# Keys and values of two attentions projected inside an earlier feed-forward and passed through DRAM

## The chip, the cores and the metric

The kernel runs on one NeuronCore of a Trainium2 chip. The metric is the time of one execution in microseconds (us) on the device, lower is better. The engines are PE (TensorE, matrix products into PSUM), ACT (ScalarE), DVE (VectorE), POOL (GpSimd) and SP (SyncE, which only issues transfers); each runs its own instructions in order and waits for others by semaphores.

## The reference, cut to what matters

Eight layers in a row change `x` (16 sequences, 128 tokens, 256 features); four of them are attentions over the same `ctx_1024` (16, 128, 256):

```python
x = x + _L0_xattn_ref(_layernorm(x), ctx_1024, ctx_1024, ...)   # autocorrelation
x = x + _L0_ffn_ref(_layernorm(x), ...)                         # quantised feed-forward
x = x + _L1_xattn_ref(_layernorm(x), ctx_1024, ctx_1024, ...)   # attention one, |i - j| <= 64
x = x + _L1_ffn_ref(_layernorm(x), ...)                         # slots
x = x + _L2_xattn_ref(_layernorm(x), ctx_1024, ctx_1024, ...)   # attention two
x = x + _L2_ffn_ref(_layernorm(x), ...)                         # receptance
x = x + _L3_xattn_ref(_layernorm(x), ctx_1024, ctx_1024, ...)   # attention three, rotary
x = x + _L3_ffn_ref(_layernorm(x), ...)                         # routed experts
# in attentions one to three, 16 heads of 16 features:
Q = query @ Wq.T + bq;  K = key @ Wk.T + bk;  V = value @ Wv.T + bv
out = softmax(Q K^T / 4) V @ Wo.T + bo     # three: Q and K turned by the rotary tables first
```

The keys and values depend on `ctx_1024` and the weights alone, not on `x`. The quantised feed-forward rounds `x`, gate, up, silu(gate) and their product each to a grid whose step needs the largest magnitude of the whole tensor.

## The kernel before, in words

Each layer is one function with one block, and a barrier of all engines stands between blocks. Inside a block every engine's instructions are written out by hand in the order in which they run; each waits on named semaphores (`enough(engine, semaphore, count)`).

`attention(layer)` serves attentions one to three. Its **preamble** computes the layer norm (a chain of small DVE instructions over all 16 sequences), and then in four groups of four sequences: keys (`project_keys`, PE; `keys_out`, ACT, or for the rotary attention `plain_out` on ACT, `swap_halves` on PE and `rope` on DVE), values (`project_values`, PE; `values_out`, DVE), and the normalised `x` turned by PE (`turn_x`) and split in two float16 parts (`x_out` on ACT, `x_low` on DVE). Then come the queries, eight jobs of 128x512 (`project_queries`, `queries_out`; rotary: the same three steps as for keys). Its **loop** takes the 16 sequences, about one per pass, in a software pipeline: PE makes approximate float16 scores for the row maxima (`maxima`), DVE reduces them, PE turns the maxima (`turn_maxima`), makes the exact float32 scores (`scores`), subtracts the maxima (`shift`), ACT takes the exponentials (`exponentials`), PE weighs the values (`weigh_values`), turns the sums, and after DVE's division turns and projects the result (`turn_sums`, `turn_attended`, `output`). Attention one adds its window to both kinds of scores with eight small matmuls each (`add_window`). DVE also adds the output bias to X (`add_bias`).

`quantised_ffn` first makes gate and up (`hidden` on PE, `evict` on ACT), then quantises. That part is a chain of three maxima over everything: up (scale US), silu (SS), product (PS). Every scale ends on DVE (`finish_scale`); ACT rounds (`round_up`, `round_silu`), DVE multiplies (`product`) and takes maxima (`max_product`), and after scale PS ACT writes `product_parts` for PE's `output`. For US, PE turns DVE's partial maxima (`combine_up_maxima`).

`slot_ffn` is the longest stage; POOL has three memsets there and nothing else.

## Time and profile before

| | us |
|---|---|
| median of 3 runs (2041.72 to 2044.39) | 2043.6 |
| the profiled execution | 2044.04 |
| its span, first to last instruction | 2042.1 |
| quantised feed-forward, 124.5 to 320.3 | 195.8 |
| attention one, 320.3 to 470.4: preamble, loop | 44.7, 104.6 |
| slots, 470.4 to 1360.9 | 890.5 |
| attention two, 1360.9 to 1494.0: preamble, loop | 42.7, 90.4 |
| attention three, 1555.8 to 1724.7: preamble, loop | 76.2, 92.7 |
| routed experts, from 1724.7 | 317.4 |

Stages follow each other without overlap, so a stage's change is the kernel's change; the median stands 0.4 us below the profiled execution, and 1.9 us of that execution lie outside its span. Times in rows are from the start of the span. "Keys" and "L851" are names and lines of the kernel before.

### The profile page before, as it was taken

What the parts mean: (1) busy time and instruction counts of PE and PEld (TensorE: products, weight loads), DVE (VectorE), ACT (ScalarE), POOL (GpSimd) and SP (SyncE); (2) the same over time, 40 slices, a digit from 0 to 9 for tenths busy, and PEclk for the clock granted to TensorE, in tenths of its full rate; (3) what the DMA queues carried; (4) which work ended last, traced back from release to release, by engine and by line L of the source; (5) the groups of instructions that cost most, each with busy time, mean ns of one, the idle gap of its engine ahead of it and who ended that gap; (6) DMA issues with size and microseconds to landing.
All of it is one profiled execution on the core that took longest, in us unless ns stands there. A gap on an engine that the chain in (4) does not pass through costs nothing. (4 is left out here: it accounts for less than half of the span.)

```text
span 2042.1 us, 40835 instructions
## 1 busy us (share of the span) xinstructions
PE 1818.8 (89%) x16076; PEld 1319.7 (65%) x16076; DVE 1502.2 (74%) x3131; ACT 1148.0 (56%) x1942; POOL 207.6 (10%) x175
## 2 busy tenths in 40 slices
PE   7959358996799999999999999988988798699997
PEld 6844145665377777766767777755665466588886
DVE  6987887667777777777777777687766777688885
ACT  3535753556366666666666665535552555377774
POOL 0001400000000000000000000000000100156664
PEclk9979779998999999999999999999998999799999
DMA  6120001002100000000000000010001001778885
GB/s 223 47 79 1 0 0 53 2 3 94 42 22 22 22 22 22 22 22 22 22 22 22 22 1 1 1 52 2 3 21 56 1 3 49 211 235 240 249 254 117
DMA packets 85037, 117.54 MB, mean 58 GB/s; under 512 B 11760, under 2 KB 70576, under 8 KB 84720
## 3 DMA queue, kind: packets, MB, share of 16 engines
q1 hardware_dynamic: 76016, 102.82, 15.6%
q0 software_dynamic: 8832, 12.11, 2.9%
q8 instruction: 130, 2.13, 0.4%
q14 instruction: 59, 0.48, 0.1%
HBM read 99.95 MB, written 14.96 MB: 56 GB/s over the span
## 5 line engine op out<-in xcount | busy, mean ns | idle before, releaser
L2637 PE MATMUL sl_ps_eo<-sl_w,sl_hT 128*128 128x256 f16 x3072 | 353.1, 273 | 0.8 <-DVE sl_hT L2880 0.7
L2614 PE MATMUL sl_ps_h<-sl_slot_inT,sl_w 128*128 128x512 f16 x1536 | 338.1, 379 | 0.5 <-ACT sl_h L2757 0.5
L2637 PEld LDWEIGHTS sl_ps_eo<-sl_w,sl_hT 128*128 128x128 f16 x3072 | 298.2, 98 | 36.1 <-DVE sl_hT L2880 1.3
L2757 ACT ACTIVATE sl_h<-sl_ps_h,sl_b1T 128x512 f32<-128x512 f32 x256 | 175.7, 687 | 170.1 <-PE sl_ps_h L2614 163.1
L2614 PEld LDWEIGHTS sl_ps_h<-sl_slot_inT,sl_w 128*128 128x128 f16 x1536 | 149.7, 98 | 176.2 <-ACT sl_h L2757 2.4
L2880 DVE TENSOR_TENSOR sl_hT<-sl_h,sl_hT 128x512 f16<-128x512 f32 x256 | 176.8, 692 | 102.2 <-ACT sl_hT L2760 97.8
L1149 DVE TENSOR_REDUCE at_neg_max<-at_ps 128x8 bf16<-128x1024 f32 x96 | 116.9, 1221 | 69.0 <-PE at_ps L831 69.0
L2143 PE MATMUL mo_ps_h<-mo_xgT,mo_w 128*128 128x256 f16 x1104 | 125.6, 274 | 5.4 <-issue 4.2
L2894 DVE SCALAR_TENSOR_TENSOR sl_result<-sl_ps_eo,sl_b 128x256 f32<-128x256 f32 x128 | 54.3, 424 | 97.7 <-PE sl_ps_eo L2637 93.4
L1224 POOL MEMSET at_v<- 128x2048 f32 x6 | 10.7, 1817 | 1123.1 <-POOLq L85 1123.1
L2154 PE MATMUL mo_ps_eo<-mo_w,mo_hT 128*128 128x256 f16 x1104 | 124.3, 273 | 0.6 <-DVE mo_y L2395 0.6
L2143 PEld LDWEIGHTS mo_ps_h<-mo_xgT,mo_w 128*128 128x128 f16 x1104 | 107.1, 98 | 21.3 <-issue 7.2
L2154 PEld LDWEIGHTS mo_ps_eo<-mo_w,mo_hT 128*128 128x128 f16 x1104 | 107.0, 98 | 12.9 <-issue 0.8
L1016 ACT ACTIVATE at_probT<-at_ps 128x1024 f32<-128x1024 f32 x96 | 98.6, 1027 | 15.8 <-PE at_ps L862 15.8
L2263 POOL DMA_INDIRECT out<-mo_y_scaled,mo_to_i x46 | 80.0, 1739 | 92.7 <-DMA out<-mo_y_scaled,mo_to_i 54.6
L2760 ACT ACTIVATE sl_hT<-sl_h 128x512 f16<-128x512 f32 x128 | 80.6, 629 | 4.0
L1023 ACT ACTIVATE at_attT<-at_ps 128x256 f32<-128x256 f32 x48 | 18.4, 383 | 110.0 <-PE at_ps L888 110.0
L2736 ACT ACTIVATE sl_combT<-sl_ps_lt 128x512 f32<-128x512 f32 x32 | 19.1, 597 | 108.6 <-PE sl_ps_lt L2593 108.6
L2218 ACT ACTIVATE mo_h<-mo_ps_h,mo_b 128x256 f32<-128x256 f32 x184 | 76.8, 476 | 4.2 <-PE mo_ps_h L2143 3.0
L1615 PE MATMUL qf_ps<-qf_xqT,qf_w_inT 128*128 128x512 f16 x288 | 66.8, 394 | 8.6 <-DVE qf_xqT L1814 6.3
L2245 POOL DMA_INDIRECT mo_xg_rows<-x_rows,mo_from_i x46 | 53.7, 1167 | 142.3 <-DVE mo_from_i L2357 125.6
L2371 DVE CAST mo_hT<-mo_h 128x512 f16<-128x512 f32 x92 | 39.3, 427 | 38.6 <-ACT mo_h L2218 38.6
(441 smaller groups left out, 3674.9 us busy)
## 6 DMA issues: line engine op xcount, KB each, us to landing
mo_w_raw<-in_L_ffn_W SPq DMA_DIRECT2D x46, 1024.0 KB, 8.7
sl_w_in<-in_L_ffn_w SPq DMA_DIRECT2D x16, 1024.0 KB, 5.5
at_ctxT<-ctx_pairs SPq DMA_DIRECT2D x9, 512.0 KB, 7.3
mo_b<-in_L_ffn_b SPq DMA_DIRECT2D x23, 128.0 KB, 4.2
ac_attention_w<-L_attention_w SPq DMA_DIRECT2D x3, 768.0 KB, 12.4
w_pairs<-ac_w_pair SPq DMA_DIRECT2D x3, 768.0 KB, 3.2
ac_ctx_all<-in_ctx SPq DMA_DIRECT2D x4, 512.0 KB, 8.2
ctx_pairs<-ac_ctx_pair SPq DMA_DIRECT2D x4, 512.0 KB, 2.6
```

Source lines behind the costliest of these rows:

```text
L1016: act.activation(probT[:, n % 2, 2 * pair:2 * pair + 2].rearrange("p r j q -> p r (j q)"), ps[:, at:at + 2], ACT.Exp, scale=SCALE).then_in ...
L1149: dve.tensor_reduce(neg_max[:, 2 * pair:2 * pair + 2, 0:HR], ps[:, at:at + 2].rearrange("p r (j k) -> p r j k", j=HR), AX.X, ALU.max, nega ...
L1615: last = pe.matmul(pair(q)[:, g], w_inT[:, w, i, k, c * P:(c + 1) * P], xqT[:, x, k, tokens], start=(k, a) == (0, 0), stop=(k, a) == (C - ...
L2143: last = pe.matmul(ps_h[:, q % 3, j % 2], w1_of(m, wp)[:, k, j * P:(j + 1) * P], xgT[:, m % 2, xp, k], start=(k, a) == (0, 0), stop=(k, a) ...
L2154: last = pe.matmul(ps_eo[:, s, 0:D], hT[:, m % 2, hp, j, s * P:(s + 1) * P], w2_of(m, wp)[:, j], start=(j, a) == (0, 0), stop=(j, a) == (H ...
L2218: act.activation(h[:, q % 2, j % 2], ps_h[:, q % 3, j % 2], ACT.Relu, bias=b1[:, m % WB, j:j + 1], scale=1.0 / W_SCALE).then_inc(h_ready, 1)
L2263: pool.indirect_dma_start(env.out, bass.IndirectOffsetOnAxis(ap=to_i[:, q:q + 1].bitcast(U32), axis=0), y_scaled[:, m % 2, s], None, compu ...
L2614: last = pe.matmul(ps_h[:, j % 2], w1[:, e % 2, w, k, j * P:(j + 1) * P], slot_inT[:, q % 2, x, k].rearrange("p b s -> p (b s)"), start=(k ...
L2637: last = pe.matmul(ps_eo[:, b % 2, 0:D], hT[:, hp, j, b * P:(b + 1) * P], w2[:, e % 2, w, j], start=(j, a) == (0, 0), stop=(j, a) == (HJ - ...
L2757: act.activation(h[:, j % 2], ps_h[:, j % 2], ACT.Gelu, bias=b1T[:, q // G4, j:j + 1], scale=1.0 / W_SCALE).then_inc(h_ready, 1)
L2760: act.activation(hT[:, 0, j], h[:, j % 2], ACT.Copy).then_inc(h_high, 1)
L2880: dve.tensor_tensor(hT[:, 1, j], h[:, j % 2], hT[:, 0, j], ALU.subtract).then_inc(h_split, 1)
```

## The change

Four things are done.

1. **Projection moves.** For attentions three and two (`PREPARED`), all keys and values are projected inside `quantised_ffn`: 32 jobs of 128x512 (`keys_values` on PE, `keys_values_out` on ACT), seven before `combine_up_maxima` and the others after it. Each goes through one of five slots to DRAM (`env.keys`, `env.values`). `round_up` starts with three instead of five.
2. **Rotation moves.** In `slot_ffn` POOL copies attention three's keys inside DRAM with halves swapped, loads both, turns them with 24 two-input instructions of 128x512 and stores them (`env.keys_roped`).
3. **Prepared preambles.** Attentions two and three load keys and values (2 MB each); POOL makes the float16 keys and adds the value bias; `x` is turned in groups around the queries.
4. **The loop of all three** is reordered; the bias of the output is added by POOL; in attention one the exact scores get no window, and POOL sets probabilities outside it to zero with four `affine_select` per sequence.

```diff
+PREPARED = (3, 2)
-UP_FIRST = 5
+UP_FIRST = 3
+KV_FIRST = 7
+KV_OUT = (7, 6, 0, 0, 2, 2, 1, 0)
...
 quantised_ffn, SP:
+            sp.wait_ge(hidden_made, 2 * PAIRS_EACH)
+            load_kv_weights(0)
+            for g in range(G4):
+                load_kv_context(g)
...
+            for j in range(KV_JOBS):
+                sp.wait_ge(kv_out, j + 1)
+                if k < C:
+                    sp.dma_start(env.keys[PREPARED[i]][:, C * g + k], kv_slots[s]).then_inc(kv_stored[s], 16)
...
 quantised_ffn, PE:
+            def keys_values(j):
+                if j == 0:
+                    pe.wait_ge(hidden_out, 2 * PAIRS_EACH)
+                pe.wait_ge(kv_w_in[i], 16)
+                pe.wait_ge(kv_ctx_in[g], 16)
+                enough(pe, kv_out, j - 5)
...
+            for j in range(KV_FIRST):
+                keys_values(j)
             combine_up_maxima()
+            for j in range(KV_FIRST, KV_JOBS):
+                keys_values(j)
             pe.wait_ge(prod_made, FC)
+            pe.wait_ge(kv_out, KV_JOBS)
             hold_clock(pe, env, ps[:, 0, 0:P], 18)
...
 quantised_ffn, ACT:
+            for j in jobs:
+                keys_values_out(j)
             act.wait_ge(scale_made, SCALE_STEPS * (PS + 1))
+            act.wait_ge(kv_made, KV_JOBS)
+            for s in range(3):
+                act.wait_ge(kv_stored[s], 16 * len(range(s, KV_JOBS, len(kv_slots))))
             for n in range(B):
                 product_parts(n)
...
 slot_ffn, POOL:
+            for job in range(JOBS):
+                pool.dma_start(key_plain, env.keys[LAYERS][:, job]).then_inc(turn_in, 16)
+                pool.dma_start(key_swap, env.keys_swapped[:, job]).then_inc(turn_in, 16)
...
+                    link(pool.tensor_tensor(four, four, table.unsqueeze(1).to_broadcast([P, 4, L]), ALU.mult))
+                link(pool.tensor_tensor(key_plain, key_plain, key_swap, ALU.add))
...
+                pool.dma_start(env.keys_roped[:, job], key_plain).then_inc(turn_out, 16)
...
 attention, PE:
             def weigh_values(n):
-                pe.wait_ge(prob_ready, 2 * (n + 1))
+                if windowed:
+                    pe.wait_ge(masked, 4 * (n + 1))
+                else:
+                    pe.wait_ge(prob_ready, 2 * (n + 1))
...
             def scores(n):
-                if windowed:
-                    add_window(first, range(R))
...
 attention, POOL:
+                pool.tensor_tensor(t.X[:, n], t.X[:, n], bo[:], ALU.add).then_inc(bo_added, 1)
...
+                    pool.tensor_copy(KT_max[:, :, 4 * g:4 * g + 4], KT[:, :, 4 * g:4 * g + 4]).then_inc(k_half, 1)
...
+                            pool.affine_select(heads, heads, pattern=[[0, 2 * HR], [-sign, P // 2]], compare_op=ALU.is_ge, fill=0.0,
+                                               base=0, channel_multiplier=sign).then_inc(masked, 1)
```

On PE, at the end of the hidden matmuls of the quantised feed-forward (`qf_ps_out<-qf_ident,qf_own_max` is the turning of up's partial maxima), before:

```order
L1615 MATMUL qf_ps<-qf_xqT,qf_w_inT 128x512 x12
L1592 MATMUL qf_ps_out<-qf_ident,qf_upT 128x128 x4
L1615 MATMUL qf_ps<-qf_xqT,qf_w_inT 128x512 x84
L1602 MATMUL qf_ps_out<-qf_ident,qf_own_max 1x128
L1605 MATMUL qf_ps_out<-qf_up_max,qf_ones_row 128x1
L55 MATMUL qf_ps<-early_ident 128x128 x18
```

and in the change (`qf_ps<-qf_xqT,qf_w_inT` of 12 are two key jobs, `qf_ps<-qf_w_inT,qf_xqT` one value job per 12):

```order
L1674 MATMUL qf_ps_out<-qf_ident,qf_upT 128x128 x4
L1697 MATMUL qf_ps<-qf_xqT,qf_w_inT 128x512 x84
L1712 MATMUL qf_ps<-qf_xqT,qf_w_inT 128x512 x12
L1719 MATMUL qf_ps<-qf_w_inT,qf_xqT 128x256 x24
L1712 MATMUL qf_ps<-qf_xqT,qf_w_inT 128x512 x12
L1719 MATMUL qf_ps<-qf_w_inT,qf_xqT 128x256 x12
L1684 MATMUL qf_ps_out<-qf_ident,qf_own_max 1x128
L1687 MATMUL qf_ps_out<-qf_up_max,qf_ones_row 128x1
L1719 MATMUL qf_ps<-qf_w_inT,qf_xqT 128x256 x12
L1712 MATMUL qf_ps<-qf_xqT,qf_w_inT 128x512 x12
```

Seven jobs, 84 matmuls, now stand between the last hidden matmul and the turning of the maxima.

On ACT, from the last sigmoid to the first product part, before (L1689 rounds up, L1693 rounds silu):

```order
L1676 ACTIVATE qf_upT<-qf_ps 128x1024 x2
L1685 ACTIVATE qf_xT<-qf_gateT,qf_scale 128x2048
L1689 ACTIVATE qf_upT<-qf_upT,qf_constant,qf_inv 128x2048 x5
L1693 ACTIVATE qf_gateT<-qf_gateT,qf_constant,qf_inv 128x2048
L1689 ACTIVATE qf_upT<-qf_upT,qf_constant,qf_inv 128x2048
L1693 ACTIVATE qf_gateT<-qf_gateT,qf_constant,qf_inv 128x2048 x5
L1697 ACTIVATE qf_xqT<-qf_gateT,qf_constant,qf_inv 128x768
L1701 ACTIVATE qf_prodT<-qf_xqT 128x768
```

and in the change, from the silu rounding on (L1804 rounds silu, L1800 rounds up, L1813 and L1816 take keys and values out):

```order
L1813 ACTIVATE qf_prodT<-qf_ps,qf_kv_bias 128x512
L1804 ACTIVATE qf_gateT<-qf_gateT,qf_constant,qf_inv 128x2048 x3
L1800 ACTIVATE qf_upT<-qf_upT,qf_constant,qf_inv 128x2048
L1813 ACTIVATE qf_w_inT<-qf_ps,qf_kv_bias 128x512
L1816 ACTIVATE qf_w_inT<-qf_ps 128x512
L1804 ACTIVATE qf_gateT<-qf_gateT,qf_constant,qf_inv 128x2048
L1800 ACTIVATE qf_upT<-qf_upT,qf_constant,qf_inv 128x2048
L1816 ACTIVATE qf_prodT<-qf_ps 128x512
L1813 ACTIVATE qf_prodT<-qf_ps,qf_kv_bias 128x512
L1804 ACTIVATE qf_gateT<-qf_gateT,qf_constant,qf_inv 128x2048
L1800 ACTIVATE qf_upT<-qf_upT,qf_constant,qf_inv 128x2048
L1813 ACTIVATE qf_prodT<-qf_ps,qf_kv_bias 128x512
```

Three silu roundings now come first, and five take-outs stand among the later roundings; fourteen more follow the last one.

On PE, one pass of attention one's loop, before (`at_window_b` the window, `at_QT_half` the approximate scores, `at_QT,at_KT` the exact ones, `at_probT,at_v` the weighing of values, `at_neg_max` the turned maxima):

```order
L838 MATMUL at_ps<-at_ident_b,at_neg_max 128x128
L812 MATMUL at_ps<-at_window_b,at_ident_b 64x4x64 x8
L831 MATMUL at_ps<-at_ctxT,at_QT_half 128x128 x16
L881 MATMUL at_ps<-early_ident,at_sumsT 128x128 x4
L895 MATMUL at_ps<-at_wo,at_attT 128x256 x2
L812 MATMUL at_ps<-at_window_b,at_ident_b 64x4x64 x8
L851 MATMUL at_ps<-at_QT,at_KT 128x256 x8
L888 MATMUL at_ps<-early_ident,at_att 128x128 x2
L862 MATMUL at_ps<-at_neg_maxT,at_slot_sel 128x128 x16
L874 MATMUL at_ps<-at_probT,at_v 32x128 x16
```

and in the change:

```order
L897 MATMUL at_ps<-at_probT,at_v 32x128 x16
L827 MATMUL at_ps<-at_window_b,at_ident_b 64x4x64 x8
L850 MATMUL at_ps<-at_ctxT,at_QT_half 128x128 x16
L912 MATMUL at_ps<-early_ident,at_att 128x128 x2
L904 MATMUL at_ps<-early_ident,at_sumsT 128x128 x4
L856 MATMUL at_ps<-at_ident_b,at_neg_max 128x16x8
L919 MATMUL at_ps<-at_wo,at_attT 128x256 x2
L870 MATMUL at_ps<-at_QT,at_KT 128x256 x8
L881 MATMUL at_ps<-at_neg_maxT,at_slot_sel 128x128 x16
```

The second window's eight matmuls are gone, the approximate scores stand directly behind the weighing, and the turning of the maxima follows that of the sums.

## Rows read from the trace of the kernel before

**Rows 1.** Windows by stage: length, busy us (instructions) per engine, PEclk, DMA share, GB/s.

```profile
365.00:469.60 104.60, 97.97 (x1714) 68.85 (x1713) 65.45 (x137) 50.34 (x81) 0.00 (x0) 1.00 0.01 2
470.40:1360.90 890.50, 861.42 (x6482) 598.40 (x6482) 650.32 (x1335) 519.69 (x961) 1.43 (x3) 0.99 0.07 23
1360.90:1403.60 42.70, 38.31 (x246) 23.06 (x247) 32.38 (x94) 21.25 (x40) 3.57 (x2) 0.96 0.19 63
1555.80:1632.00 76.20, 60.32 (x292) 31.59 (x292) 54.40 (x116) 37.22 (x68) 11.92 (x9) 0.91 0.12 38
```

**Rows 2.** Timeline, quantised feed-forward, PE: start, us, instruction, idle before, releaser.

```profile
217.50 2.75 PE L1615 MATMUL qf_ps<-qf_xqT,qf_w_inT 128*128 128x512 f16 x12 [0.35 <-ACT qf_upT L1676]
233.80 0.37 PE L1602 MATMUL qf_ps_out<-qf_ident,qf_own_max 128*1 128x128 f32 x1 [13.55 <-DVE qf_own_max L1793]
```

**Rows 3.** Windows inside the quantised feed-forward, columns as in the first group.

```profile
224.00:228.00 4.00, 0.00 (x0) 0.00 (x0) 3.97 (x2) 1.85 (x1) 2.37 (x2) 0.68 0.00 0
272.00:276.00 4.00, 3.58 (x17) 3.58 (x17) 4.00 (x3) 0.00 (x0) 0.00 (x0) 0.50 0.00 0
```

**Rows 4.** DMA issues: queue, count, KB each, median us to landing.

```profile
sl_hT<-in_L_ffn_slot_embeds SPq DMA_DIRECT2D x1, 1024.0 KB, 5.6
ctx_pairs<-ac_ctx_pair SPq DMA_DIRECT2D x4, 512.0 KB, 2.6
```

**Rows 5.** Timeline of the quantised feed-forward, ACT, then DVE.

```profile
235.75 10.04 ACT L1689 ACTIVATE qf_upT<-qf_upT,qf_constant,qf_inv 128x2048 f32<-128x2048 f32 x5 [9.89 <-DVE qf_inv L1803]
246.40 2.09 ACT L1693 ACTIVATE qf_gateT<-qf_gateT,qf_constant,qf_inv 128x2048 f32<-128x2048 f32 x1 [0.62 <-DVE qf_inv L1803]
278.21 1.03 ACT L1697 ACTIVATE qf_xqT<-qf_gateT,qf_constant,qf_inv 128x768 f32<-128x768 f32 x1 [17.81 <-DVE qf_inv L1803]
252.50 2.29 DVE L1833 TENSOR_TENSOR qf_gateT<-qf_gateT,qf_upT 128x2048 f32<-128x2048 int16 x1 [1.68 <-ACT qf_gateT L1693]
```

**Rows 6.** Timeline of one iteration of attention one's loop, PE, then ACT.

```profile
405.70 0.23 PE L838 MATMUL at_ps<-at_ident_b,at_neg_max 128*128 128x128 bf16 x1
408.37 0.62 PE L812 MATMUL at_ps<-at_window_b,at_ident_b 64*64 64x256 bf16 x8
410.70 1.08 PE L874 MATMUL at_ps<-at_probT,at_v 128*32 128x128 f32 x32
411.71 0.23 PE L838 MATMUL at_ps<-at_ident_b,at_neg_max 128*128 128x128 bf16 x1
410.82 1.02 ACT L1016 ACTIVATE at_probT<-at_ps 128x1024 f32<-128x1024 f32 x1
```

**Rows 7.** Timeline, POOL twice, then the DVE instruction beside the second.

```profile
196.77 1.88 POOL L1562 TENSOR_SCALAR qf_xT<-qf_xT 128x2048 f32<-128x2048 f32 x1 [7.49 <-issue]
216.52 3.83 POOL L1564 TENSOR_SCALAR qf_sig_more<-qf_sig_more 128x2048 f32<-128x2048 f32 x1
215.17 3.41 DVE L1824 SCALAR_TENSOR_TENSOR qf_gateT<-qf_sig_more,qf_gateT 128x2048 f32<-128x2048 f32 x1
```

**Rows 8.** Timeline of attention two's preamble, DVE, then ACT.

```profile
1366.64 1.38 DVE L1098 TENSOR_SCALAR at_xn_ring<-X,at_meanvar,at_rstd 128x256 f32<-128x256 f32 x4
1377.73 0.42 DVE L1134 TENSOR_TENSOR at_xT<-at_ps,at_xT 128x256 f16<-128x256 f32 x1 [0.21 <-ACT at_xT L1005]
1378.39 0.42 DVE L1134 TENSOR_TENSOR at_xT<-at_ps,at_xT 128x256 f16<-128x256 f32 x1
1371.12 1.21 ACT L1005 ACTIVATE at_xT<-at_ps 128x256 f16<-128x256 f32 x4 [2.27 <-PE at_ps L802]
1392.34 10.93 ACT L990 ACTIVATE at_QT<-at_ps,at_bq_parity,at_parity_scale 128x512 f32<-128x512 f32 x16 [2.29 <-PE at_ps L760]
```

**Rows 9.** Timeline of attention three's preamble, ACT, then PE.

```profile
1575.33 0.60 ACT L1001 ACTIVATE at_xn_ring<-X,at_shift_x,at_rstd 128x256 f32<-128x256 f32 x1
1576.08 0.60 ACT L1001 ACTIVATE at_xn_ring<-X,at_shift_x,at_rstd 128x256 f32<-128x256 f32 x1
1604.96 4.15 PE L760 MATMUL at_ps<-at_xT,at_wT 128*128 128x512 f16 x12 [0.98 <-issue]
```

416 lines of the change are left out of this document (266 added, 150 removed).

## The prediction

> **What bounds the kernel now.** I read the windows by stage first [rows 1], because a barrier ends every stage: only a stage that gets shorter makes the kernel shorter. The slots are PE's stage (861 of 890.5 us busy), and so is attention one's loop (98.0 of 104.6). There, work that is taken from PE counts and work for other engines is hidden. The two preambles that lose their keys and values are chains: PE 38.3 of 42.7 us in attention two, 60.3 of 76.2 in attention three, with DVE and ACT long behind it. The quantised feed-forward I then read in the timeline of each engine, since it is a chain with holes. PE ends its last hidden matmuls at 217.50 + 2.75 = 220.25 and stands idle for 13.55 us until it turns up's maxima at 233.80 [rows 2]; ACT idles 9.89 us before it rounds up and 17.81 us before the first product part at 278.21 [rows 5]. The new work goes into these holes. The windows show also that PE's clock is not full there: granted 0.68 while it is idle at 224 to 228, and 0.50 (1.2 of 2.4 GHz) at 272 to 276 though it is busy [rows 3].
>
> **Quantised feed-forward: +9 us.** A matmul group of 12 takes 2.75 us at full clock [rows 2]; two key jobs are 12 such matmuls (one value job has the same columns), so a job is 1.375 us at full clock and 2.75 at half. SP starts the loads only when the hidden matmuls have ended, at 220.25: weights and the first contexts, estimated 1 MB, and a 1 MB load has landed 5.6 us after its issue [rows 4]. So PE starts at 225.9. A mean of 0.68 over 224 to 228 is full clock for 1.4 us and half for the rest, so it fell at about 225.4, just before. I take the first 4 us at half clock (1.5 jobs) and 5.5 jobs at full: 4 + 7.6, and the seven end at 237.5. Up's maxima are turned 3.7 us later than at 233.80. Bounds: all at full clock 235.5 (+1.7), all at half 245.2 (+11.4).
>
> ACT takes seven jobs out in its idle 9.89 us, rounds up three times (2.0 each, a fifth of 10.04) and takes six jobs out at 0.68 us, the price of a 128x512 query take-out [rows 8]. From 239.5 that ends at 249.6, when scale SS comes (246.40 + 3.7 = 250.1). DVE's product then no longer waits the 1.68 us [rows 5] for a rounding of up that stood between two of silu, so scale PS comes at 278.2 + 3.7 − 1.7 = 280.2. But ACT has from 250.1 six roundings of silu, three of up at 2.0 to 2.1, and five take-outs, 21.4 us, until 271.5, and fourteen take-outs behind them. PE can hold six results ahead, so from the first freed bank at 272.2 it still has eight jobs: 11.0 us, and 2 more for a clock that fell meanwhile, 285.2. Then the last take-out, 0.7, and its store, because the first product part waits for it (its tile is the slots'): 2.6 as for a store of 512 KB [rows 4]. That makes 288.5 against 278.21, +10. With no clock loss and a store of half that it is +7; with eight jobs at half clock, +19 (with the late bound of the maxima instead, +18). I take **+9**, between the first two.
>
> **Attention one's loop: −4 us.** One pass is 6.01 us (405.70 to 411.71) [rows 6]. PE loses the second window, 0.62, and gains little: the turning of the maxima, which stood behind the weighing at 411.71, must now have POOL's selects, whose input, the first exponential half, ends at 410.82 + 1.02 = 411.84; I put 0.2 for it. So 5.6 a pass, −6 over 15 passes, and +2 for the last sequence, where two selects stand in the chain. POOL has in each pass the bias and four selects of 64x512 elements; no row has a select. By one-input rows of 2048 elements [rows 7] 512 elements are 0.47 us alone (1.88 / 4) and 0.96 beside DVE (3.83 / 4). I take 0.9 with its wait, and 0.6 for the bias: 4.2 us, below 5.6, so PE keeps the loop. At 0.47 nothing is different; at 0.96 it is 4.4, still below. Loops of attentions two and three lose no matmuls; reordered waits are given and taken: 0 ± 2.
>
> By the Trainium skill, page "GPSIMD Engine Reference", section "3.1 Elementwise — side-by-side cycle accounting", a two-input operation of 2048 float32 elements takes 4497 ns on GpSimd, an estimated 1.12 us for 512. By that a pass of POOL would be about 5.1 us, still under PE's, and the sum would stay as it is. Section "4.1 Engine selection" puts elementwise adds and products on VectorE, at about half the time; that speaks against this change, and decides only where POOL is waited for.
>
> **Slots: +3.5 us (0 to +26).** POOL copies 2 × 1 MB inside DRAM while the stage's constants load, and turns the keys by 24 two-input operations. PE waits for constants only at the start, so I put 2.4 us there. DVE's two-input operation beside POOL took 3.41 us where 2.29 is its time without [rows 5, 7]: 24 × 1.1 = 26 us of DVE if all collide and nothing covers it. DVE is busy 650 of 890.5 us and PE has 29 us without work [rows 1], so I take 1.1.
>
> **Attention two's preamble: −12.5 us (−6 to −15).** The norm ends as before at 1366.64; four sequences of normalised x end 1.4 later. Two groups of x at 0.66 a sequence (1377.73 to 1378.39) are 5.3, up to 1373.3, and preparing the queries 0.7. Queries start at 1374.1 instead of some 2 us ahead of 1392.34; their take-outs last 10.93, eight x_outs at 0.30 stand among them (2.4), and 2 to 3 go to waits and a colder PE [rows 8]. The loop starts near 1391, not 1403.6. If PE runs at half clock, −6; with no waits at all, −15. Keys and values (2 MB each, by the 1 MB row about 11 us each) are issued at the stage's start and needed only in the loop.
>
> **Attention three's preamble: −25 us (−18 to −33).** The norm ends 5.9 us into the stage as in attention two, at 1561.8; four normal_x 2.1; two groups at 0.75 a sequence (1575.33 to 1576.08) 6.0; ready at 1571 where queries start at 1604.96 now [rows 9]. From there the preamble lasts 27.1 us (1604.96 to its end at 1632.0). To this come the two groups of x among the queries, 4 × 0.75 + 4 × 0.4 = 4.6, DVE's rotary products beside POOL's value bias, 3, and the clock, 1: 1606.7, 25.3 earlier. If neither x nor POOL costs PE time, the end is 1571 + 27.1, −33; if POOL costs DVE twice as much and PE runs the queries at half clock (+4), −18.
>
> **Sum.** +9 − 4 + 0 + 3.5 − 12.5 − 25 = −29. Against the profiled execution's 2044.04: **2015.0 us** (the same sum on the median, 0.4 lower, is 2014.6).
>
> **Rivals.** *GpSimd bounds attention one (slower).* If a select takes 1.15 us, POOL's pass with bias and hand-overs (1.4) is 6.0 us and the loop gains nothing; at 1.55 it is 7.6, the loop loses 16 × 1.6 = 25 us, all that the other parts bring, and the kernel is even; at 2.0 us it is 9.4, the loop loses 54, and the time is 2044 − 25 + 54 = 2073. For it: no row shows a select, and each waits for the one before it. Against it: 512 elements in one-input rows are 0.47 to 0.96. The same page of the Trainium skill, in section "3.1", estimates nothing for a select itself; no run here shows one.
>
> *The quantised stage stays at the lower clock.* All seven early jobs and the later ones at 2.75 us give +19 to +25 there instead of +9, with up to 6 us more in the preambles: 2025 to 2037, centre 2031. For it: 0.50 granted at 272 to 276 though PE is busy [rows 3]. Against: the projection is longer uninterrupted work than the 3.58 us there.
>
> *All is covered.* The fourteen last take-outs overlap scale PS (+7 in place of +9), slots at 0, attention three at −31: 2004. For it: PE's 29 idle us in the slots.
>
> *Transfers are late.* Keys and values (4 MB) are read in both preambles at the time of x's own constants; if the loads are all in only 22 us after a stage's start, and POOL's four float16 copies of 1024 elements then take 8 (half of 3.83 each, [rows 7]) and the first maxima 3, attention two's loop starts at 1360.9 + 33 = 1394, 3 later than above; if attention three's x waits for the same queue 10, its −25 is −15: 2028. That would be the change not doing what it says: the same wait for keys, from DRAM instead of PE.
>
> **How the numbers follow.** The forecast has 0.60, with its own range of 2005 to 2026; all covered 0.14, the lower clock 0.10, late transfers 0.08, GpSimd as the bound 0.08. The range, 1998 to 2040, takes in all but the last and the far ends of the sums. Within 0.2% (4 us) is about what a measurement here can't tell from no change; only a GpSimd rival near its even point falls there, 0.02, and some of the lower clock. Faster 0.89, same 0.03, slower 0.08.
>
> **What would show it.** Right: the seven key jobs between 225.9 and 237.5; a first product part near 288; passes of attention one at 5.6 us with POOL idle in each; 894 us of slots; loops starting 30 and 51 us into attentions two and three. Wrong: a row of selects above 1.2 us with PE waiting for POOL; DVE waiting for POOL's float16 keys at the first maxima; PE at 0.5 through the whole of the quantised tail.

## The result and the profile after

Five runs of the changed kernel took 2015.01 to 2027.28 us, median **2015.54**, against 2043.29 before on the same chip (2041.72 to 2044.39): ratio **0.988** (95% interval 0.985 to 0.991). The profiled execution took 2015.01, its span is 2013.3. In the rest of the text the span is divided as follows: a stage ends with PE's last filler matmul in it, a loop begins with the first turning of maxima (the table is worked out from the timelines of PE; its marks lie up to 2 us beside those of the table shown before).

| stage | before | after | change | predicted |
|---|---|---|---|---|
| first attention (autocorrelation) | 122.4 | 123.2 | +0.8 | 0 |
| quantised feed-forward | 196.6 | 202.0 | +5.4 | +9 |
| attention one, preamble | 45.9 | 45.4 | −0.5 | 0 |
| attention one, loop | 104.3 | 98.3 | −6.1 | −4 |
| slots | 889.6 | 902.7 | **+13.1** | +3.5 |
| attention two, preamble | 44.8 | 37.2 | −7.6 | −12.5 |
| attention two, loop | 89.6 | 87.6 | −2.0 | 0 |
| receptance | 60.4 | 61.4 | +1.0 | 0 |
| attention three, preamble | 78.4 | 51.6 | −26.8 | −25 |
| attention three, loop | 91.5 | 86.2 | −5.3 | 0 |
| routed experts | 318.6 | 317.8 | −0.8 | 0 |
| sum | 2042.1 | 2013.3 | **−28.8** | −29 |

That the sum was hit so closely is luck: errors of up to 9.6 us in single stages cancelled. Stages whose code no run touched scatter: over all thirteen profiles with the change or a variant of it attention one's preamble took 45.3 to 46.9, receptance 58.5 to 62.0, routed experts 315.0 to 321.0, and the three loops, where their code was that of the changed kernel, 96.5 to 100.1, 86.0 to 87.9 and 86.0 to 89.3. So a difference of 2 to 3 us in a stage, or of several in a single time, is no finding by itself. The kernel before, too, had medians of 2040.4 to 2048.9 on the chips on which the experiments ran. The experiments are therefore read by the stage that they touch, and inside it by what waits for what.

Windows of the changed kernel, columns as in [rows 1]: attention one's loop, slots, the two preambles, then a stretch of the quantised feed-forward that answers to the second of [rows 3].

```profile
370.60:469.20 98.60, 86.58 (x1574) 65.60 (x1574) 63.33 (x121) 52.26 (x81) 53.58 (x80) 0.97 0.01 2
469.90:1373.80 903.90, 866.13 (x6482) 600.41 (x6482) 660.90 (x1336) 520.37 (x961) 51.20 (x56) 0.98 0.10 32
1373.80:1408.80 35.00, 20.09 (x103) 10.36 (x103) 28.39 (x75) 16.47 (x32) 21.05 (x23) 0.80 0.40 143
1559.90:1609.30 49.40, 29.62 (x133) 14.51 (x133) 36.14 (x76) 27.67 (x56) 29.42 (x30) 0.79 0.30 105
...
271.00:279.00 8.00, 7.93 (x50) 4.84 (x51) 7.69 (x6) 5.89 (x10) 0.14 (x1) 1.00 0.78 291
```

In the first row PE is busy 86.6 us instead of 98.0: the matmuls of one of the two windows are gone (128 in all), and POOL has 53.6 us that it did not have. In the second PE has as many matmuls as before and DVE one instruction more, yet PE is busy 4.7 us longer, DVE 10.6, and 13 us more go by: the same instructions take longer. The preambles are granted a mean clock of 0.80 and 0.79, where it was 0.96 and 0.91. In the quantised tail (last row) PE is at full clock, where [rows 3] had 0.50.

The timeline of the quantised feed-forward in the changed kernel, answering to [rows 2, 5] (start, us, instruction, idle before, releaser): PE's first key job and the turning of up's maxima, the end of scale PS on DVE, the first product part on ACT.

```profile
227.03 4.12 PE L1712 MATMUL qf_ps<-qf_xqT,qf_w_inT 128*128 128x512 f16 x12 [5.95 <-DMA qf_xqT<-ctx_pairs]
237.50 0.27 PE L1684 MATMUL qf_ps_out<-qf_ident,qf_own_max 128*1 128x128 f32 x1
...
279.63 0.16 DVE L1939 TENSOR_TENSOR qf_inv<-qf_inv,qf_unit 128x1 f32<-128x1 f32 x1
...
284.47 1.03 ACT L1820 ACTIVATE qf_xqT<-qf_gateT,qf_constant,qf_inv 128x768 f32<-128x768 f32 x1 [2.19 <-DMA values<-qf_prodT]
```

The stage starts 0.8 us later than before. The key jobs start at 227.03, predicted 225.9; the first 12 matmuls, two jobs, take 4.12 us where [rows 2] has 2.75 for 12, so they begin at the lower clock; the maxima are turned at 237.50. (The seven jobs ahead of them are 60 matmuls, not 84 as the description of the change has it; the prediction reckons by jobs, so nothing in it changes.) Scale PS ends at 279.8, and ACT begins the product parts 4.7 later, after 2.19 us of waiting for the last store.

The timeline of one pass of attention one's loop, answering to [rows 6]: POOL's selects and bias, then two successive weighings on PE.

```profile
405.82 1.38 POOL L1266 TENSOR_SCALAR_AFFINE_SELECT at_probT<-at_probT 64x512 f32<-64x512 f32 x2 [1.40 <-issue]
...
408.94 0.73 POOL L1237 TENSOR_TENSOR X<-X,at_bo 128x256 f32<-128x256 f32 x1 [0.17 <-POOL at_probT L1266]
...
409.93 1.08 PE L897 MATMUL at_ps<-at_probT,at_v 128*32 128x128 f32 x32
415.18 1.08 PE L897 MATMUL at_ps<-at_probT,at_v 128*32 128x128 f32 x32
```

A select takes 0.69 (1.38 / 2), a pass 415.18 − 409.93 = 5.25 us where it was 6.01. POOL idles 1.40 in this pass and is not the bound.

The DMA issues at the start of the slots, behind the "..." that of the constants in the kernel before: queue, count, KB each where known, median us to landing.

```profile
keys_swapped<-keys POOLq DMA_DIRECT2D x2, 10.4
sl_b_rows<-in_L_ffn_b SPq DMA_DIRECT2D x1, 32.0 KB, 11.6
...
sl_b_rows<-in_L_ffn_b SPq DMA_DIRECT2D x1, 32.0 KB, 5.7
```

The timeline in the slots, first DVE, then POOL, then PE: a wait for the constants, and the first turning of keys.

```profile
485.23 0.17 DVE L3076 TENSOR_SCALAR sl_w_scale<-sl_gamma_col 128x2 f32<-128x2 f32 x1 [9.16 <-DMA sl_b_rows<-in_L_ffn_b]
...
523.29 1.48 DVE L3041 CAST sl_hT<-sl_h 128x512 f16<-128x512 f32 x1
524.80 1.63 DVE L3043 TENSOR_TENSOR sl_hT<-sl_h,sl_hT 128x512 f16<-128x512 f32 x1
526.36 1.28 DVE L3002 TENSOR_REDUCE sl_row_max<-sl_ps_eo 128x1 f32<-128x512 f32 x2
...
530.83 0.69 DVE L3043 TENSOR_TENSOR sl_hT<-sl_h,sl_hT 128x512 f16<-128x512 f32 x1
...
521.02 3.47 POOL L2966 TENSOR_TENSOR sl_xn<-sl_xn 128x512 f32<-128x512 f32 x2 [5.06 <-DMA sl_xn<-keys_swapped]
524.57 1.32 POOL L2967 TENSOR_TENSOR sl_xn<-sl_xn 128x512 f32<-128x512 f32 x1
...
527.18 1.87 PE L2704 MATMUL sl_ps_eo<-sl_slotsT,sl_xrT 128*128 128x512 f16 x4 [4.29 <-DVE sl_row_max L3002]
...
532.28 1.19 PE L2704 MATMUL sl_ps_eo<-sl_slotsT,sl_xrT 128*128 128x512 f16 x4 [0.44 <-DVE sl_row_max L3002]
```

Two things are to be seen. The constants `sl_b_rows` land after 11.6 us beside the copies of keys (5.7 in the kernel before), and DVE waits 9.16 for them (1.59 before). And while POOL turns keys (521.02 to 525.89), DVE's cast takes 1.48 and the subtraction behind it 1.63; without POOL the subtraction takes 0.69 (530.83), the cast 0.42. The row maxima, which read PSUM, take 1.28 for two as always. PE waits 4.29 us for them, and behind the wait its four matmuls take 1.87, where four such take 1.19 a little later: PE comes out of the wait at the lower clock (0.50 granted at 527 to 529).

The timeline at attention two's first queries, answering to [rows 8]: DVE's constants, POOL's casts, PE; and, behind the last "...", PE's first queries of attention three, answering to [rows 9].

```profile
1387.56 0.86 DVE L1098 TENSOR_SCALAR at_parity_scale<-early_parity_of_row 128x2 f32<-128x2 f32 x1
...
1389.38 0.97 DVE L1104 CAST at_slot_sel<-early_slot_of_row 128x512 bf16<-128x512 f32 x1
...
1385.27 4.12 POOL L1243 CAST at_ctxT<-at_KT 128x1024 f16<-128x1024 f32 x4 [7.94 <-DMA at_bv<-L_attention_bv]
...
1390.46 4.37 PE L778 MATMUL at_ps<-at_xT,at_wT 128*128 128x512 f16 x12 [6.02 <-issue]
...
1577.51 4.70 PE L778 MATMUL at_ps<-at_xT,at_wT 128*128 128x512 f16 x12 [5.22 <-issue]
```

Five small DVE instructions (two of them shown) last 2.9 us beside POOL's casts of keys, and the first queries start 16.7 us into the stage.

### The profile page after: what moved, and what is told of

It is laid out like the page before. It is cut to its first block and busy times, and to the rows that moved or that the text cites. A ratio compares the mean times of both kernels' runs of the same rounds, so it can differ in the third digit from the quotient of the medians.

```text
span 2013.3 us, 40727 instructions
## 1 busy us (share of the span) xinstructions
PE 1799.9 (89%) x15896; PEld 1320.4 (66%) x15896; DVE 1480.2 (74%) x3023; ACT 1156.9 (57%) x1954; POOL 371.2 (18%) x379
## 5 line engine op out<-in xcount | busy, mean ns | idle before, releaser
L3043 DVE TENSOR_TENSOR sl_hT<-sl_h,sl_hT 128x512 f16<-128x512 f32 x256 | 181.1, 709 | 98.8 <-ACT sl_hT L2900 94.5
L2890 ACT ACTIVATE sl_slot_inT<-sl_ps_in 128x512 f16<-128x512 f32 x64 | 38.1, 597 | 50.4 <-PE sl_ps_in L2742 50.0
L2512 DVE TENSOR_TENSOR mo_hT<-mo_h,mo_hT 128x512 f16<-128x512 f32 x92 | 63.8, 694 | 3.1
```

The lines of the kernel that those rows point to most:

```text
L3043: dve.tensor_tensor(hT[:, 1, j], h[:, j % 2], hT[:, 0, j], ALU.subtract).then_inc(h_split, 1)
```

## Experiments

One theory was stated against the table: **the slots lose 5 us at their start, to the copies, and 8 us to POOL turning keys where PE depends on DVE; preambles lose 5 us to DVE's constants.** Its rival was that the 13 us are spread over the whole stage or come from the clock. To read this, I set the mark of an event in a run against the same event before, both counted from the stage's first matmul (before: first slot logits 16.18, row maxima turned 73.83, first combination 82.54). This lag behind before is, in us:

| kernel | logits | maxima turned | first combination | end of stage |
|---|---|---|---|---|
| changed kernel | 5.28 | 9.43 | 11.10 | 13.30 |
| no turning work | 4.68 | 6.40 | 6.40 | 6.40 |
| copies later | 0.90 | 6.70 | 10.68 | 15.84 |
| turning after the maxima | 5.34 | 5.18 | 7.27 | 11.81 |
| turning after a first result | 3.79 | 4.94 | 4.93 | 8.14 |
| turning in quarters | 4.98 | 6.08 | 8.30 | 8.30 |
| combined | 3.44 | 4.35 | 4.35 | 6.37 |
| same slots code (six other profiles) | 3.6 to 5.2 | 9.5 to 15.6 | 10.9 to 19.6 | 13.2 to 22.9 |

The last row is important: the loss with unchanged code varies from 13 to 23 us, and one profile of an edited kernel is to be held against all of it. Of the six kernels that change what POOL does there, or when, all but copies-later end below that row, turning after the maxima by 1.4 us only.

**1. The turning without its operations** (`no_turn_work`). The 24 operations are left out; loads and stores of the keys stay, so attention three gets unturned keys.

```diff
-                link = Links(pool, turn_link, 3, job)
...
-                for tile, table in ((key_plain, key_cos), (key_swap, key_sin)):
-                    four = tile.rearrange("p (b l) -> p b l", l=L)
-                    link(pool.tensor_tensor(four, four, table.unsqueeze(1).to_broadcast([P, 4, L]), ALU.mult))
-                link(pool.tensor_tensor(key_plain, key_plain, key_swap, ALU.add))
-                link.done()
```

> This leaves out the 24 multiplications and additions that turn attention three's keys; their loads and stores stay, so attention three scores with unturned keys. Theory (POOL's operations slow DVE): the lag between the first slot logits and the end of the stage goes from 7.8 us to under 1, the kernel takes 2008. Rival (the 24 transfers of POOL's queue, or their issue, cost the time): the lag stays above 5 and the kernel at 2013 to 2015.

2003.78 us, slots 896.1. The 8.0 us behind the logits (8.0 to 19.3 with unchanged code) fall to 1.7; under 1 was expected. DVE's windows over the first 84 us of turning, in the changed kernel:

```profile
521.00:605.00 84.00, 65.09 (x101) 0.94 0.27 91
```

and in this one, whose stage began 2.9 us earlier:

```profile
521.00:605.00 84.00, 60.67 (x113) 0.98 0.27 92
```

DVE does 113 instructions instead of 101, and is busy 4.4 us less, in a stretch in which PE waits for it; DMA moves as much. It is the operations, not their transfers.

**2. The copies later** (`copies_late`).

```diff
+            pool.wait_ge(row_split, NT)
             for half in range(2):
                 pool.dma_start(swapped(env.keys_swapped, half), swapped(env.keys[LAYERS], 1 - half)).then_inc(swap_out, 16)
-            pool.wait_ge(row_split, NT)
```

> Theory: the 5.3 us at the start of the slots are constants that land late because two copies of 1 MB inside DRAM share the DMA engines with them; with the copies behind the split rows the first slot logits come 16.2 us after the stage's first matmul as before, not 21.5, and the kernel takes 2010. Rival: the constants are late for another reason (the stage issues them in the order of before), and the start stays at 21.5 us, the kernel at 2015.

2022.72 us, slots 905.2. The DMA issue of the constants in this run:

```profile
sl_b_rows<-in_L_ffn_b SPq DMA_DIRECT2D x1, 32.0 KB, 4.1
```

They land after 4.1 us and the lag at the logits is 0.9, so the copies make the constants late, and that costs the start over 4 us. (Experiment 12 has a lag of 3.4 there without the copies, with PE at the lower clock; so this cause is read from the landing, not from the lag alone.) But the turning loses 15 us from the logits to the stage's end, as it does in some executions of unchanged code (8.0 to 19.3), and the kernel is no faster. The start was confirmed, the time forecast for the kernel was not.

**3. Turning only after all row maxima** (`rotate_late`).

```diff
             pool.wait_ge(swap_out, 32)
+            pool.wait_ge(rmax_ready, 2 * B + 1)
             for job in range(JOBS):
```

> The slots of the change take 902.7 us, before 889.6: +13.1, of which 5.3 stand before the first slot logits, 5.8 up to the first combination and 2.0 while POOL still turns keys; behind that the lag is constant. Theory: the last two parts, 7.8 us, are POOL's two-input work slowing DVE while PE waits for DVE's row maxima; if POOL starts to turn only when those maxima are made, DVE has slack and the slots become 895 us, the kernel 2007.5. Rival: POOL slows DVE wherever it runs and DVE has no slack: the slots stay near 902 and the kernel at 2015.

2013.15 us, slots 901.5. Up to the maxima nothing is lost any more (5.18 against 5.34 at the logits), but 6.6 us in the steps behind them. The timeline there, DVE, then PE, and last PE's first combination in the kernel before:

```profile
577.97 1.75 DVE L3044 TENSOR_TENSOR sl_hT<-sl_h,sl_hT 128x512 f16<-128x512 f32 x1 [0.55 <-ACT sl_hT L2900]
579.65 1.49 DVE L3042 CAST sl_hT<-sl_h 128x512 f16<-128x512 f32 x1
...
560.23 0.49 PE L2764 MATMUL sl_ps_out<-sl_result_parts,sl_comb_parts 128*128 128x257 f16 x3 [2.92 <-DVE sl_result_parts L3063]
...
583.58 2.76 PE L2754 MATMUL sl_ps_h<-sl_slot_inT,sl_w 128*128 128x512 f16 x12 [1.61 <-ACT sl_h L2897]
...
552.98 0.49 PE L2624 MATMUL sl_ps_out<-sl_result_parts,sl_comb_parts 128*128 128x257 f16 x3 [0.83 <-DVE sl_result_parts L2899]
```

The chain of the first result hangs on DVE too: PE waits 2.92 for it at the first combination, where it waited 0.83 before the change, and later 1.61 for ACT, which itself had waited 1.73 for DVE, where it did not wait before. DVE's subtraction and cast take 1.75 and 1.49. The theory that the row maxima are the one sensitive place fell: the steps behind them, in which PE waits for DVE, are another.

**4. Turning only after the first result is stored** (`rotate_later`).

```diff
             pool.wait_ge(swap_out, 32)
+            pool.wait_ge(out_made, 16)
             for job in range(JOBS):
```

> POOL begins to turn the keys only after 16 combinations, some 120 us after the row maxima. With the start right behind the maxima the slots still took 901.5 us: nothing was lost in the maxima, but 6.7 us in the two steps behind them. Theory: what decides is whether PE waits for DVE in the step that POOL falls in; in the steps from the fifth on DVE has slack, so only the 5.3 us of the late constants stay and 0 to 1 more: slots 895 to 896, kernel 2007 to 2008. Rival: POOL's operations cost PE in every step, and the slots stay above 899.

2011.77 us, slots 897.5. Nothing is lost up to the eighth combination (lag still 4.94), and 3.2 us while POOL turns, at 659 to 751 us. That lies between the two forecasts: a later place is cheaper, but in the steady part it is not free, though PE is then nearly always busy.

**5. Turning in quarters** (`small_turns`). The same products and sums in 96 instructions of 128x128.

```diff
-                    four = tile.rearrange("p (b l) -> p b l", l=L)
-                    link(pool.tensor_tensor(four, four, table.unsqueeze(1).to_broadcast([P, 4, L]), ALU.mult))
...
+                    for b in range(4):
+                        part = tile[:, b * L:(b + 1) * L]
+                        link(pool.tensor_tensor(part, part, table, ALU.mult))
...
```

> The 24 operations that turn the keys become 96 of a quarter of the columns (128x128), at the place where the change has them. Beside an operation of 1.3 us DVE's cast of 128x512 took 1.48 us instead of 0.42, its subtraction 1.63 instead of 0.69: about one POOL operation more. Theory: a DVE instruction that reads two operands or casts from SBUF waits until POOL's running instruction is over; with quarters of about 0.35 us none of them takes over 0.45 us longer, and the lag that the slots gather between the first logits and their end falls from 8 us (or the 13 to 19 of other executions) to 3 to 5. Rival: the two engines share the reads in proportion and DVE's instructions become as long as before (casts of 1.2 us and more), with the lag at 8 or above.

2008.60 us, slots 897.7. The timeline at the first key job, DVE beside POOL, DVE without it, then POOL:

```profile
522.40 0.68 DVE L3044 CAST sl_hT<-sl_h 128x512 f16<-128x512 f32 x1
523.12 0.83 DVE L3046 TENSOR_TENSOR sl_hT<-sl_h,sl_hT 128x512 f16<-128x512 f32 x1
...
531.44 0.42 DVE L3044 CAST sl_hT<-sl_h 128x512 f16<-128x512 f32 x1
531.89 0.69 DVE L3046 TENSOR_TENSOR sl_hT<-sl_h,sl_hT 128x512 f16<-128x512 f32 x1
...
520.72 5.66 POOL L2967 TENSOR_TENSOR sl_xn<-sl_xn 128x128 f32<-128x128 f32 x8 [5.01 <-DMA sl_xn<-keys_swapped]
526.46 3.24 POOL L2970 TENSOR_TENSOR sl_xn<-sl_xn 128x128 f32<-128x128 f32 x4
```

Beside quarters the cast takes 0.68 and the subtraction 0.83, where 1.48 and 1.63 stood; the loss behind the logits is 3.3 us instead of 8.0, although POOL's own time rose (8.9 us against 4.8 for the first job). So what DVE loses follows the length of POOL's single instruction. The ends of the instructions show how. In the slots of the changed kernel, shown above, POOL's second product ends at 521.02 + 3.47 = 524.49, its sum at 524.57 + 1.32 = 525.89; DVE's cast ends 0.28 behind the first, at 524.77, and its subtraction 0.54 behind the second, at 526.43. So it is in all twelve profiles in which POOL turns keys: all 39 casts `sl_hT<-sl_h` that are stretched end 0.28 to 0.29 us behind the end of an instruction of POOL, all 78 stretched subtractions 0.54 to 0.55, though they took between 0.61 and 1.80. In the kernel before none of either is stretched (0.41 to 0.43, 0.68 to 0.69). The DVE instruction waits until POOL's running one ends; the rival, two engines that share the reads in proportion, would give no such constants. Which resource it waits for, no run tells. By the Trainium skill, page "GPSIMD Engine Reference", section "8. Key points", GpSimd shares its SBUF interfaces with VectorE, with contention for instructions of DVE with two SBUF inputs or in a two-port mode; the trace agrees for the subtraction (0.69 to 1.63), and shows it for the cast with one input too (0.42 to 1.48); whether that cast runs in a two-port mode no run tells.

**6. DVE's constants before x** (`prepare_first`).

```diff
-                dve.wait_ge(consts_in, CONSTS)
+                if not prepared:
+                    dve.wait_ge(consts_in, CONSTS)
...
+            prepare()
             if prepared:
                 for g in range(2):
                     x_group(g)
-                prepare()
+                dve.wait_ge(consts_in, CONSTS)
```

> In attentions two and three DVE makes its five constants ahead of the turned x. Theory: these five took 3 us, not 0.7, because POOL makes the float16 keys at that time, and PE's queries wait for them: first queries 16.7 us (attention two) and 17.7 us (three) after the stage's start become 11.6 and 14, the preambles shorten by 5 and 3.5 us, the kernel takes 2007. Rival: the preambles are bound by POOL's own chain (float16 keys, value bias) or by the key loads; the queries start earlier but the loops start within 1 us of now, kernel 2014 to 2015.

2007.66 us. The timeline in attention two, DVE's first and last constant, and PE's first queries:

```profile
1381.81 0.10 DVE L1099 TENSOR_SCALAR at_parity_scale<-early_parity_of_row 128x2 f32<-128x2 f32 x1
...
1382.03 0.42 DVE L1105 CAST at_slot_sel<-early_slot_of_row 128x512 bf16<-128x512 f32 x1
...
1386.47 4.74 PE L778 MATMUL at_ps<-at_xT,at_wT 128*128 128x512 f16 x12 [0.66 <-DMA at_bv<-L_attention_bv]
```

The constants cost 0.10 to 0.42 each now, while POOL stands idle (its casts begin at 1386.48), the queries start 4.0 us earlier although this stage began 0.9 later, and the preambles are 4.7 and 2.4 us shorter, where 5 and 3.5 were expected. It is the casts of POOL, 1.03 each (4.12 / 4), that stretched them: an instruction with two elements a partition went from 0.86 to 0.10. The edit also takes the constants out of the queries' chain, so the 4.7 are not the stretching alone.

**7. The quantised tail** (`qf_tail`). Two more of the jobs are taken out ahead of scale PS, and the turn of the five slots is shifted, so that the last store isn't from a slot that the product parts write.

```diff
-KV_OUT = (7, 6, 0, 0, 2, 2, 1, 0)
+KV_OUT = (7, 6, 0, 0, 2, 3, 2, 0)
...
-                s = j % len(kv_slots)
+                s = (j + 3) % len(kv_slots)
```

> Two of the fourteen take-outs behind the last rounding move ahead of it, and the tiles of the slots are taken in another turn, so that the last two stores go from tiles that no product part overwrites. Theory: scale PS is ready at 279.8, only 0.9 later than before, and the first product part (284.5) waits 4.7 us for the take-outs and the last store: it comes 4 us earlier, the kernel takes 2011.5. Rival: the seven early jobs, which turn up's maxima 2.9 us later, are what the stage lost, and rounding waits again for DVE; the first product part comes less than 1.5 us earlier.

2018.82 us, this stage 200.6. PE's first key jobs, the end of scale PS on DVE, the first product part on ACT:

```profile
227.98 5.28 PE L1712 MATMUL qf_ps<-qf_xqT,qf_w_inT 128*128 128x512 f16 x12 [6.38 <-DMA qf_xqT<-ctx_pairs]
...
282.13 0.16 DVE L1939 TENSOR_TENSOR qf_inv<-qf_inv,qf_unit 128x1 f32<-128x1 f32 x1
...
283.40 1.03 ACT L1820 ACTIVATE qf_xqT<-qf_gateT,qf_constant,qf_inv 128x768 f32<-128x768 f32 x1 [0.16 <-DMA keys<-qf_prodT]
```

The first product part follows scale PS by 1.1 us instead of 4.7, as the theory had it. But the first 12 matmuls took 5.28 instead of 4.12 (at the lower clock again), and up's maxima were turned at 239.99, 2.1 later in the stage. The stage gained 1.4 of 3.6, in its size what the rival had said, though not for the rival's reason; in experiment 12, with the same edit and maxima 0.4 earlier in the stage than in the changed kernel, it gained 3.4.

**8. Keys and values of attention three alone** (`only_three`).

```diff
-PREPARED = (3, 2)
+PREPARED = (3,)
...
-KV_OUT = (7, 6, 0, 0, 2, 2, 1, 0)
+KV_OUT = (7, 6, 0, 0, 1, 1, 1, 0)
```

> Only attention three's keys and values are projected early: 16 jobs, and attention two projects its own again, in the new order. Theory: fourteen take-outs behind the last rounding become almost none, so the quantised feed-forward takes 197 to 198.5 instead of 202.0 (the maxima's 0.9 stays), attention two's preamble 44.5 to 45 instead of 37.2; the slots, loops and attention three as with both: about 3 us more in all, 2015.3 + 3.5 = 2019, or as much above the other kernel of this chip. Rival: the quantised feed-forward does not get shorter, because the seven early jobs set its length, and the kernel loses all of attention two's 7.6 us.

2020.65 us. The quantised feed-forward gives back 4.7 us of its 5.4, attention two's preamble is 45.0, as before the change. Net, by these two stages: preparing attention two is worth 3.0 us, as was expected. Another 2.6 us of the difference are in slots with unchanged code; the other stages go up and down by up to 3.1 and cancel.

**9. The output bias on DVE again** (`bias_on_dve`).

```diff
+                if n < B:
+                    dve.tensor_tensor(t.X[:, n], t.X[:, n], bo[:], ALU.add).then_inc(bo_added, 1)
...
-                add_bias(n)
```

> In all three attentions DVE adds the bias again, between the row maxima and the division, as before. Theory: the loops became shorter (5.07 to 4.73 us a pass in two and three) because PE's rows stand in an order with less idle time between them, and DVE has 0.9 us idle in a pass: loops of two and three change by less than 1 us each (87.6, 86.2), that of one too (98.3). Rival: DVE is in the ring of waits (maxima, division, turning); 0.4 us more a pass gives back most of it: 5.0 us a pass, +4 each, the kernel 2023 to 2027.

2026.81 us, of which slots (unchanged code) have 5.9 more than in the changed kernel. Weighings of two successive passes, in the loops of attentions one and two:

```profile
405.77 1.08 PE L897 MATMUL at_ps<-at_probT,at_v 128*32 128x128 f32 x32 [0.39 <-issue]
411.21 1.08 PE L897 MATMUL at_ps<-at_probT,at_v 128*32 128x128 f32 x32 [0.39 <-issue]
...
1452.23 1.08 PE L897 MATMUL at_ps<-at_probT,at_v 128*32 128x128 f32 x32 [0.20 <-issue]
1457.12 1.08 PE L897 MATMUL at_ps<-at_probT,at_v 128*32 128x128 f32 x32 [0.16 <-issue]
```

Passes take 5.44 and 4.89 us, 5.25 and 4.70 with the bias on POOL; attention two's pass was 5.07 before the change. So 0.19 of the 0.37 that a pass gained there is the bias, and the other half is left for the new order. This lies between the two forecasts (4.73 and 5.0 a pass). The median pass is the same within 0.01 us in every profile with the same loop; the loops as wholes, 1.3, 1.0 and 2.3 us longer here, vary by that much or more at their start and end.

**10. The window in the exact scores again** (`window_in_scores`), instead of POOL's selects.

```diff
+                if windowed:
+                    add_window(lambda r: ring_bank(first, r))
...
-                                  start=c == 0, stop=False, skip_group_check=True)
+                                  start=c == 0 and not windowed, stop=False, skip_group_check=True)
...
-                    pe.wait_ge(masked, 4 * (n + 1))
```

> Attention one gets its second window back (eight matmuls of 0.62 us a pass) and loses POOL's selects. Theory: of the 0.76 us that a pass became shorter (6.01 to 5.25) 0.62 are the window and the rest the order; a pass takes 5.85 and the loop 106 us, less 2 at its end, where no select stands in the chain of the last sequence. Rival: most of the gain is the order and the window hides in waits for the exponentials: a pass below 5.5, the loop below 101.

2029.24 us. Two successive weighings on PE:

```profile
409.20 1.08 PE L896 MATMUL at_ps<-at_probT,at_v 128*32 128x128 f32 x32
415.01 1.08 PE L896 MATMUL at_ps<-at_probT,at_v 128*32 128x128 f32 x32
```

A pass is 5.81 us: 0.56 of the 0.76 gained come from the window with its selects, and attention one's loop is 104.0, as before the change. The slots, unchanged, take 912.5, which makes the time look worse than the edit is.

**11. The changed kernel once more** (`after_again`), five rounds, unedited but for a blank line at its end.

> The changed kernel itself, once more and beside the next kernel. Five earlier times of it lie at 2015.0 to 2015.5 three times, at 2023.9 and 2027.3 twice, and the slots took 902.6 to 912.5 us in four profiles in which their code was this one. Theory: the spread is POOL's turning meeting DVE's row maxima at another moment in each execution; times between 2013 and 2030, no two groups that agree within 0.3%. Rival: it was chance of that chip; all five times within 4 us.

2013.03 to 2024.20 us in six runs, ratio 0.989 (0.987 to 0.991). The result repeats, and so does the spread. But the kernel before, eleven times on the same chip, spread over 9.1 us too (2037.78 to 2046.85), so the spread alone does not show that it comes from POOL.

**12. What helped, together** (`combined`): `prepare_first`, `qf_tail`, and copies and turning behind the first result.

```diff
+            pool.wait_ge(row_split, NT)
+            pool.wait_ge(out_made, 16)
             for half in range(2):
                 pool.dma_start(swapped(env.keys_swapped, half), swapped(env.keys[LAYERS], 1 - half)).then_inc(swap_out, 16)
-            pool.wait_ge(row_split, NT)
```

> Four edits together: copies inside DRAM and turning behind 16 combinations of the slots, DVE's constants first in attentions two and three, two take-outs earlier and the last stores from free tiles in the quantised feed-forward. By the runs so far: slots 894 (start as before, 3 to 4 us for the turning in steps with slack), preambles 32.5 and 49.2, quantised feed-forward 198 to 200.5: 2015.3 - 9 - 7 - 3 = 1996, and by the theory on the spread the five times lie within 6 us of each other, not 12. Rival: PE's clock and POOL's turning find other stages to slow; above 2005, with a spread as wide as the changed kernel's.

**1995.41 us** (1994.59 to 1999.43), ratio to before **0.978** (0.977 to 0.980): it beats both kernels. Quantised feed-forward 198.7, slots 896.0, preambles 31.7 and 47.9. Turning costs 2.0 us there; the start still lags by 3.44, though the copies are gone. PE's filler matmuls at the start of the slots, in this run:

```profile
479.11 3.73 PE L56 MATMUL sl_ps_eo<-early_ident 128*128 128x128 f32 x16
```

and in the run with the copies later:

```profile
483.64 2.00 PE L56 MATMUL sl_ps_eo<-early_ident 128*128 128x128 f32 x16
```

Sixteen take 3.73 us against 2.00: PE was at the lower clock in one and not in the other, though the code ahead in this stage is the same. Why, stays open.

## Why the prediction was right, and where only in sum

**Quantised feed-forward, +9 for +5.4.** The mechanism stands. Up's maxima came 2.9 us later (+3.7 were forecast, in which too much lower clock was put on the first jobs; PE waited 5.95 for the loads, as 5.6 said). Scale PS came 0.8 later (2.0 forecast). The mis-sized term is the tail behind it, 4.7 instead of 8.3: its eight jobs lost nothing to the clock (1.00 granted at 271 to 279), and the store cost 2.19, not 2.6. Experiment 7 shows where the 4.7 lay. The rival with the lower clock did not come to pass, though a single execution lost 1.2 us to it in the first jobs (experiment 7).

**Attention one's loop, −4 for −6.1.** PE stayed the bound, as forecast. The steady pass is 5.25 and not 5.6: experiments 9 and 10 split its gain of 0.76 into 0.56 for the window, where 0.62 − 0.2 stood, and 0.19 for the bias that left DVE, for which nothing stood. That selects are 0.69 and not 0.9 changes nothing there, since POOL is not waited for long. Against this stands the end: 11.5 us from the last weighing to the stage's end, 6.6 before, +4.9 where +2 was put. So the fifteen passes brought 9.1 and the end took back half of it; the forecast of 4 came close by two misses of opposite sign. The rival with GpSimd as the bound would have needed 1.15 us for a select.

**Loops two and three, 0 ± 2 for −2.0 and −5.3.** The step "reordered waits are given and taken" failed: passes are 0.3 to 0.4 shorter, half of it because DVE no longer adds the bias. The gain is cut by a longer drain: in attention two 10.2 us lie between the last weighing and the end (8.6 in eleven of the twelve other profiles), 6.6 before.

**Slots, +3.5 for +13.1: the step that failed.** For the 2.4 at the start 5.3 were measured, for the 1.1 of the collisions 8.0; over 4 of the first go with the copies (experiment 2), 6.3 of the second with POOL's operations (experiment 1; 3 to 5 agree). The error was to let PE's share of the whole stage cover DVE: "DVE is busy 650 of 890.5 us" is true, but POOL turned keys at 521 to 605 us, where PE waits for DVE's maxima. The price per collision, 1.1, taken from other instructions in [rows 5, 7], came near (the subtraction loses 0.94, the cast 1.06), but as it follows POOL's instruction and not DVE's (experiment 5), that was luck; the cover was not looked up in its place. What the sum did not have here is PE's clock: behind such a wait PE ran at the lower one (0.50 granted at 527 to 529). The upper bound of 26 held: no profile of unchanged slots code lost over 23, start included.

**Attention two, −12.5 for −7.6.** Queries start 16.7 us into the stage, 13.2 were forecast. "Preparing the queries 0.7" was 2.9: the price of instructions that ran alone was used beside POOL's casts, although the slots' term had the collision in it. With these instructions ahead of the casts and of x (experiment 6) the preamble is at −12.3.

**Attention three, −25 for −26.8.** Queries start at 17.6, 2.4 later than forecast, mainly for the same reason (the five instructions last 2.9 here too); the rest lasted 31.8, not 35.7. Two misses of opposite sign. The forecast's own start does not add up: by [rows 8] the norm ends 5.7 into the stage, not 5.9, and the terms named end at 1569.9, where 1571 was used.

**Late transfers and "all is covered"** fell: no row of PE in the two loops waits for keys or values, and neither slots nor the quantised tail hid their work.

**What stays open.** Why unchanged slots lose 13 in one execution and 23 in another. A part of it is the clock. PE's windows (length, PE busy, granted clock, DMA) over the 130 us that begin 20 us after the stage's first matmul, in the changed kernel and in `window_in_scores`, which lost most:

```profile
489.90:619.90 130.00, 105.17 (x677) 0.92 0.23 81
494.90:624.90 130.00, 100.23 (x603) 0.87 0.22 77
```

The kernel before has 0.95 there, and in the seven profiles of unchanged slots code the figure falls from 0.92 to 0.87, roughly as the loss grows. A mean lower by 0.05 is 13 us more at the lower of two levels (0.05 × 130 / 0.5), in which PE does work for half of them: an estimate of at most 6.5 of the 9.6 us that this execution lost more. The rest are longer waits of PE. Whether other collisions lower the clock, or the clock shifts the collisions, is not shown. The combined kernel, whose turning is out of the sensitive stretches, spreads over 4.8 us where the changed one spread over 12.3 and 11.2; that supports collisions that fall differently each time, but the kernel before, without any, spread over 9.1 in eleven runs, and no execution at the long end of the changed kernel's spread was profiled. Of the reordered loops two and three only the bias was undone by itself; the rest of the new order was not taken apart.

## What to carry to other kernels

An engine's share of a whole stage hides nothing in particular: look up which engine is waited for in the very stretch in which the new work will run, and put the work where that engine has slack. In this kernel work on GpSimd was charged to VectorE too, where VectorE cast or combined what lies in SBUF, by what was left of GpSimd's running instruction: cut such instructions, or place them away from VectorE's chains, small constants included. When a prediction of the sum comes true, compare it by stage before trusting its terms; here 9.6 and 4.9 us too little in two places were made up by 3.6 in the quantised stage, 2.1 in attention one and 9.1 in attentions two and three's other parts.

## What had not been expected of the hardware

- A cast from SBUF on DVE, with one input, is held up by POOL as much as an operation with two (0.42 to 1.48, 0.69 to 1.63 beside 128x512 on POOL); reductions that read PSUM are not (1.28 to 1.29 for two, also beside POOL). With POOL's instructions cut to a quarter the same two take at most 0.68 and 0.95. Whatever the length, the cast ends 0.28 to 0.29 and the subtraction 0.54 to 0.55 behind the end of POOL's instruction.
- Two copies of 1 MB inside DRAM delay a load of 32 KB that another queue issued from 5.7 to 11.6 us.
- PE's filler matmuls at the start of a stage run at half the rate in some executions and not in others (3.73 against 2.00 us for sixteen); without the copies the slots' first logits came 2.5 us later in the execution with the slow ones (a lag of 3.44 against 0.90), while `prepare_first`, with 3.73 and the copies, lags no more than the rest (5.2).
